# One change to a causal attention and int8 FFN layer on eight cores: how the last chunk of queries is cut, and what stands in its tail

## The reference, cut to what matters

```python
# x: (16, 2048, 1024) float32, 16 heads of 64
Q, K, V = heads(x @ WQ.T), heads(x @ WK.T), heads(x @ WV.T)
attn = softmax(where(causal, Q @ K.T / 8, -1e9)) @ V
x = layernorm(x + merge(attn) @ WO.T)            # eps 1e-5, over 1024
n = x * rsqrt(mean(x * x) + 1e-6)
q = clip(round(n * 127 / absmax(n)), -128, 127) * absmax(n) / 127   # per row
y = layernorm(x + (q @ (w_int8 * weight_scale).T + bias))
```

## Time and profile before

| | us |
|---|---|
| median of 3 runs (lowest, highest) | 1003.89 (1002.97, 1004.13) |
| the profiled execution's own time | 1004.11 |
| its span, slowest core (core 2) | 1002.6 |
| the other cores' spans | 994.9 to 1001.9 |

### The profile page before, as it was taken

How to read it: one execution, slowest core, us unless ns; L and a number is a source line. 1 busy time by engine, 2 the same in 40 slices (tenths; PEclk the granted TensorE clock), 3 DMA queues, 4 the chain that set the end, 5 groups by cost and what they waited for, 6 DMA issues and landing times.

```text
span 1002.6 us, 22536 instructions; the slowest of 8 cores (994.9 to 1002.6 us)
## 1 busy us (share of the span) xinstructions
PE 907.1 (90%) x8267; PEld 409.9 (41%) x8416; DVE 519.0 (52%) x1263; ACT 687.2 (69%) x713; POOL 227.4 (23%) x290
## 2 busy tenths in 40 slices
PE   3894999999999989999999999999799999999863
PEld 1342444444444433434444444444344444444421
DVE  0110147744786327653127747762477523776675
ACT  0133666776877789999744566777577779999931
POOL 5021322231122121221223232232122211222101
PEclk9997999999999999999999999999899999999897
DMA  9999333250223141221154251144413210114212
GB/s 117 146 178 182 65 45 42 64 147 13 28 64 101 54 53 28 79 44 62 37 66 66 64 148 23 33 107 94 49 33 102 74 44 10 25 26 146 62 56 63
DMA packets 99289, 71.18 MB, mean 71 GB/s; under 512 B 70384, under 2 KB 88816, under 8 KB 99184
## 3 DMA queue, kind: packets, MB, share of 16 engines
q1 hardware_dynamic: 78368, 50.87, 20.5%
q0 software_dynamic: 20816, 18.88, 14.8%
HBM read 55.05 MB, written 16.78 MB: 72 GB/s over the span
## 4 chain that ended last, share of the span: by engine, by line
PE 77%; DMA 8%; ACT 6%; issue 3%; DVE 3%; POOL 1%; DVEq 0%; POOLq 0%; ACTq 0%; SPq 0%
PE ps L324 47%; PE ps L640 16%; PE ps L531 14%; ACT PT L559 5%; DMA WV<-wvt 4%; DMA QO<-OS 2%; DMA XT<-xt 1%; DVE OS L682 1%; DMA QT<-QB 1%; POOL PT L574 1%; ACT Q L844 1%; POOL WK L148 0%; POOL WQ L148 0%; DVE SM L678 0%; DVE Z L749 0%
## 5 line engine op out<-in xcount | busy, mean ns | idle before, releaser
L559 ACT ACTIVATE PT<-ps,SM 128x1024 bf16<-128x1024 f32 (+2 forms) x576 | 586.2, 1066 | 151.8 <-PE ps L531 149.8
L574 POOL TENSOR_TENSOR PT<-PT,MASK 128x256 bf16<-128x256 bf16 (+1 forms) x184 | 158.2, 867 | 506.0 <-ACT PT L559 505.8
L640 PE MATMUL ps<-VX,PT 128*128 128x65 bf16 x4352 | 235.1, 195 | 25.4 <-DVE OS L682 22.6
L640 PEld LDWEIGHTS ps<-VX,PT 128*128 128x128 bf16 x4352 | 179.2, 98 | 177.0 <-issue 141.9
L531 PE MATMUL ps<-QO,KT 64*128 64x512 bf16 (+1 forms) x1504 | 193.3, 325 | 10.9 <-ACT PT L559 10.2
L324 PE MATMUL ps<-XT,WK 128*128 128x512 bf16 x486 | 126.0, 386 | 23.8 <-DMA XT<-xt 22.4
L324 PE MATMUL ps<-W,QT 128*128 128x512 bf16 x477 | 128.6, 385 | 17.5 <-DMA QT<-QB 13.8
L324 PE MATMUL ps<-WO,QO 128*128 128x512 bf16 x474 | 127.0, 378 | 4.2 <-issue 1.7
L324 PE MATMUL ps<-XT,WQ 128*128 128x512 bf16 x485 | 124.6, 380 | 2.5 <-DMA WQ<-wqt 1.1
L324 PE MATMUL ps<-WV,XT 128*128 128x512 bf16 x489 | 124.1, 383 | 2.7 <-DMA WV<-wvt 1.4
L531 PEld LDWEIGHTS ps<-QO,KT 64*128 64x128 bf16 x1504 | 51.7, 94 | 182.2 <-issue 177.3
(11 more groups left out here) (50 smaller groups left out, 546.5 us busy)
## 6 DMA issues: line engine op xcount, KB each, us to landing
Z<-x SPq DMA_DIRECT2D x32, 512.0 KB, 4.4
y<-Z SPq DMA_DIRECT2D x32, 512.0 KB, 2.8
XT<-xt POOLq DMA_DIRECT2D x7, 1024.0 KB, 12.5
WK<-wkt POOLq DMA_DIRECT2D x4, 512.0 KB, 21.4
WQ<-wqt POOLq DMA_DIRECT2D x4, 512.0 KB, 24.6
WV<-wvt POOLq DMA_DIRECT2D x2, 1024.0 KB, 42.2
WO<-wot POOLq DMA_DIRECT2D x1, 2048.0 KB, 70.6
W<-w8t POOLq DMA_DIRECT2D x1, 2048.0 KB, 87.1
```

What stands on the lines that cost most here:

```text
L559: emit("s", lambda eng: eng.activation(dst, src, AF.Exp, bias=EB, scale=0.125).then_inc(sem["s"], 1))
L574: emit("g", lambda eng: eng.tensor_tensor(blk, blk, msk, ALU.mult).then_inc(sem["m"], 1))
L640: last = eng.matmul(ps[:, o_at + s_ * o_head + q * 65: o_at + s_ * o_head + q * 65 + 65], PT[:, pt0 + s_ * 512 + c0: pt0 + s_ * 512 + c0 + ...
```

## The change

1. **Last chunk.** Chunk 7 becomes three stretches: 256, 128 and 128 queries. In a stretch of 128, a unit has four keys' blocks against 128 queries: S is 8 matmuls of 128 columns instead of 4 of 256. Such a stretch has 4 units for each pair of heads, 32 in all, so the chunk keeps 56 + 64 units. Its diagonal unit is the new kind `f`. The `ffn` and `wo` of tile 30 now also stand in the list of chunk 7, behind those of 28 and 29; only tile 31 is left for the tail.
2. **Fillers.** The list of chunk 7 is in another order, and its work is divided over 16 gaps fewer.
3. **Half-tile statistics, in all chunks.** BN_STATS, maximum and minimum of a half are put into `bg` as soon as that half of `wo` is done (`z_half`), and likewise BN_STATS of a half of `ffn` (`y_half`). Some of the planner's costs change (750 to 690, 1400 to 1200, 1100 to 350 + 160 nq).
4. **Last tile.** Its last scaling is done in two halves, one on ACT and one on DVE, with a store for each.
5. **Unread matmuls.** In the tail, PE gets 12 matmuls of 128x512 before tile 31's `wo` and 45 before its `ffn`; they write the score buffer and nobody reads them.

```diff
-        subs += [(NCH - 1, 0, 2), (NCH - 1, 2, 2)]
+        subs += [(NCH - 1, 0, 2), (NCH - 1, 2, 1), (NCH - 1, 3, 1)]
...
+                    kinds = ["f"] + list(range(first_k % 4, first_k, 4))
...
+            if nq == 1:
+                keys = ([k0] + list(range(k0 % 4)) if kd == "f"
+                        else list(range(kd, kd + 4)))
+                return [(k, j * 128, q0 * 128, 128)
+                        for j, k in enumerate(keys)]
...
-            dve_load(1100.0)
+            dve_load(350.0 + 160.0 * nq)
...
+        def z_half(n, j):
+            z = zt(n, j * 512, j * 512 + 512)
...
+            for f in (stats, high, low):
+                bg.append((690.0, lambda f=f: emit("v", f)))
...
-            part(0)
-            part(1)
...
-            if on_act:
+            if n == 4 * NCH - 1:
+                wait("s", tok_sm2[n])
+                emit("s", lambda eng: eng.activation(
+                    zt(n, 0, 512), zt(n, 0, 512), AF.Identity,
+                    bias=sm(n, 32, 33), scale=sm(n, 31, 32)).then_inc(
+                        sem["s"], 1))
+                t0 = bump("s")
+                wait("v", tok_sm2[n])
+                emit("v", lambda eng: eng.tensor_scalar(
+                    zt(n, 512, 1024), zt(n, 512, 1024), sm(n, 28, 29),
+                    sm(n, 31, 32), ALU.subtract, ALU.mult).then_inc(
+                        sem["v"], 1))
+                store(n, bump("v"), 512, 1024)
+                store(n, t0, 0, 512)
+            elif on_act:
...
+                if g == NCH - 1:
+                    order = [wo[0], wo[1], ff[0], wo[2], ff[1], wo[3],
+                             ff[2], ff[3]]
...
-                mine += behind([4 * g, 4 * g + 1])
+                mine = (mine[:4] + carry[:2] + mine[4:6] + carry[2:]
+                        + mine[6:])
+                carry = []
+                mine += behind([4 * g, 4 * g + 1]) + behind([4 * g + 2])
...
-            gaps = [todo]
+            gaps = [2 * len(pairs[g]) - (16 if g == NCH - 1 else 0)]
...
-        main.extend(behind([4 * NCH - 2, 4 * NCH - 1]))
+        main.extend(behind([4 * NCH - 1]))
+        def warm():
+            if idle[0] == 0:
+                wait("t", tok_exp[len(units) - 1], tok_exp[len(units) - 2])
+            idle[0] += 1
+            emit("t", lambda eng: eng.matmul(
+                ps[:, 0:512], WO[:, 0:128], WO[:, 0:512], start=True,
+                stop=True, skip_group_check=True))
         while main or st["open"] or timed or bg:
             if step() == 0.0:
-                spend(100.0)
+                if main and idle[0] < (12 if len(main) > 2 else 57):
+                    warm()
+                    spend(216.0)
+                else:
+                    spend(100.0)
```

More of the change, by code:

```diff
@@ L483, in build_nc @@
                     kinds = ["d0", "d1", "d2"] + list(range(first_k))
+                elif nq == 2:
+                    kinds = ["e"] + list(range(0, first_k, 2))
                 else:
-                    kinds = ["e"] + list(range(0, first_k, 2))
+                    kinds = ["f"] + list(range(first_k % 4, first_k, 4))
                 for kd in kinds:
@@ L551, in emit_s @@
             s0 = (u % 2) * 1024
-            if kd in ("d2", "e"):
-                c0, nc_ = (256, 256) if kd == "d2" else (0, 384)
+            if kd in ("d2", "e", "f"):
+                c0, nc_ = {"d2": (256, 256), "e": (0, 384),
+                           "f": (0, 128 * len(mm))}[kd]
                 dst = ap(PT, pt0 + c0, (4096, 128), (512, 2), (1, nc_))
@@ L586, in pv_lists @@
                 return [(k0, 1, 128)], [(k0, 0, 0), (k0 + 1, 1, 256)]
+            if nq == 1:
+                if kd == "f":
+                    return ([(k, 0, 128 + k * 128) for k in range(k0 % 4)],
+                            [(k0, 0, 0)])
+                return [(kd + j, 0, j * 128) for j in range(4)], []
             if nq == 2:
@@ L698, in o_out @@
             if hp == 7:
-                later(5500.0, lambda: state["ot_all"].add(su))
+                later(5500.0 if su < len(subs) - 1 else 3800.0, lambda: state["ot_all"].add(su))
         tok_x, tok_store, tok_sm, tok_q16, tok_qt8 = {}, {}, {}, {}, {}
@@ L713, in sm, with rows @@
             return SM[:, s0 + c0:s0 + c1]
-        def rows(t_h, n):
+        def rows(t_h, n, c0=0, c1=D):
             g, r = n // 4, n % 4
-            return ap(t_h, (g // 4) * S * D + ((g % 4) * 512 + r * 128) * D,
-                      (D, 128), (1, D))
+            return ap(t_h, (g // 4) * S * D + ((g % 4) * 512 + r * 128) * D
+                      + c0, (D, 128), (1, c1 - c0))
         def x_load(n):
@@ L752, in done @@
                 tok = bump("v")
+                z_half(n, dc)
                 if dc == 1:
@@ L758, in wo_filler, with stats, high, low @@
                           pieces, done)
+        def z_half(n, j):
+            z = zt(n, j * 512, j * 512 + 512)
+            def stats(eng):
+                eng.drain()
+                eng.bn_stats(sm(n, 16 + 6 * j, 22 + 6 * j), z)
+            def high(eng):
+                eng.tensor_reduce(sm(n, 2 + j, 3 + j), z, AX.X, ALU.max)
+            def low(eng):
+                eng.tensor_reduce(sm(n, 4 + j, 5 + j), z, AX.X, ALU.min)
+            for f in (stats, high, low):
+                bg.append((690.0, lambda f=f: emit("v", f)))
         def z_stats(n):
@@ L767, in col @@
                 return sm(n, j, j + 1)
-            def part(j):
-                z = zt(n, j * 512, j * 512 + 512)
-                def stats(eng):
-                    if j == 0:
-                        eng.drain()
-                    eng.bn_stats(sm(n, 16 + 6 * j, 22 + 6 * j), z)
-                def high(eng):
-                    eng.tensor_reduce(col(2 + j), z, AX.X, ALU.max)
-                def low(eng):
-                    eng.tensor_reduce(col(4 + j), z, AX.X, ALU.min)
-                for f in (stats, high, low):
-                    bg.append((750.0, lambda f=f: emit("v", f)))
-            part(0)
-            part(1)
             def f(eng):
@@ L912, in done @@
                 tok = bump("v")
+                y_half(n, dc)
                 if dc == 1:
@@ L918, in ffn_filler, with y_half, f @@
                           pieces, done)
-        def y_stats(n):
-            def part(j):
-                def f(eng):
-                    if j == 0:
-                        eng.drain()
-                    eng.bn_stats(sm(n, 16 + 6 * j, 22 + 6 * j),
-                                 zt(n, j * 512, j * 512 + 512))
-                bg.append((750.0, lambda: emit("v", f)))
-            part(0)
-            part(1)
+        def y_half(n, j):
+            def f(eng):
+                eng.drain()
+                eng.bn_stats(sm(n, 16 + 6 * j, 22 + 6 * j),
+                             zt(n, j * 512, j * 512 + 512))
+            bg.append((690.0, lambda: emit("v", f)))
+        def y_stats(n):
             def f(eng):
@@ L976, in store @@
             emit("y", lambda eng: eng.dma_start(
-                rows(y_h, n), zt(n)).then_inc(sem[key], 16))
+                rows(y_h, n, c0, c1), zt(n, c0, c1)).then_inc(sem[key], 16))
             tok_store[n] = bump(key, 16)
@@ L1095, in build_nc @@
             carry = late
-            todo = 2 * len(pairs[g])
-            gaps = [todo]
+            gaps = [2 * len(pairs[g]) - (16 if g == NCH - 1 else 0)]
             def gap():
@@ L1115, in build_nc @@
         pv_pair(npair - 1, gap)
-        main.extend(behind([4 * NCH - 2, 4 * NCH - 1]))
+        main.extend(behind([4 * NCH - 1]))
+        idle = [0]
+        def warm():
[5 more added lines that the diff above has]
+                stop=True, skip_group_check=True))
         while main or st["open"] or timed or bg:
             if step() == 0.0:
-                spend(100.0)
+                if main and idle[0] < (12 if len(main) > 2 else 57):
[3 more added lines that the diff above has]
+                    spend(100.0)
         for n in range(4 * NCH - NZ, 4 * NCH):
```

11 lines of the change are left out of this document (6 added, 5 removed).

## The result

The changed kernel is slower. Its median is 1010.7 us (5 runs), against 1003.66 us for five runs of the kernel before on the same chip. The ratio of the two is 1.0071, with a 95% interval of 1.0056 to 1.0085. The forecast was 1001.3 with a range of 996.5 to 1006.5: the sign and the range are both wrong. An interval stands in brackets. One of the five executions took 1101.72 us, with the cores of one die at a lower clock; such executions occur with and without the change, and they are counted in the medians here and in no ratio.

A forecast was written before the change was run, and what follows sets the result against it. PE and ACT nearly full in the last chunk, then a chain of dependent steps in the tail. Span 1002.6 - 13.8 (tail) + 11.7 (chunk 7) - 0.5 (statistics) = 1000.0, as a median 1001.3 us, range 996.5 to 1006.5.

The forecast's parts named there:

- Tail: After the last PV matmul: tile 31 alone remains, so the tail takes 29.3 us instead of 43.1, a gain of 13.8.
- Unread matmuls: In the tail: they hold the clock before tile 31's `ffn`, which without them would pay 3.2 us.
- Chunk 7: Last chunk: 48 moved filler matmuls cost 10.4 us, units without filler +0.8, clock 0.5; chunk longer by 11.7.
- the step that made +0.8: Chunk 7: PE time lost in units without filler, rising from 23 to 30, goes from 4.3 to 5.1 us.
- The 0.5 for the clock: Chunk 7: 0.5 us added for low clock around the longest row without filler, bounds 0 and 5.6.
- Narrow S, masks, head pairs at 0: Chunk 7: S in 128-column matmuls and eight more head pairs with masks and divisions add nothing.
- narrow S is bound by its instructions: Rival, chunk 7: S pays per instruction, +0.43 us on 38 units, 16 us; 1017 us, chance 0.02.
- the chunk swallows all of it: Rival, chunk 7: PE bound and narrow S dearer than wide; at 0.2 us per S 1008.9 us, chance 0.11.
- Half-tile statistics at -0.5, bounds -2 and +2: All chunks: DVE executes the same instructions, divisions stand less long behind statistics; -0.5 us in 72 head pairs.
- Cold tail: Rival, tail: unread matmuls come at half clock, 19 us, past the 11.8 when `ffn` is ready; +7, 1008 us, chance 0.05.
- No change: Rival, chunk 7: excess of 1 to 3 us from low clock or `ffn` queued before its transpose; 1003.5 us, chance 0.18.
- the chunk hides the work: Rival, chunk 7: the new order fills idle time counted as lost, chunk grows by 8; 997.5 us, chance 0.16.

The follow-up runs named there:

- e8: The changed kernel without the 57 unread matmuls in the tail; ratio 1.0110 to the kernel before, tail 34.0 us.
- e3: The changed kernel with half-tile statistics undone (both halves after the second `wo` half) and the old planner costs; ratio 1.0011 to the kernel before.
- e14: The changed kernel with half-tile statistics and changed planner costs only from chunk 7 on; ratio 1.0036 to the kernel before.
- e4: The kernel before with only chunk 7 cut into 256, 128 and 128 queries, last transpose estimate 3800 instead of 5500; ratio 1.0061, chunk 7 136.4 us.
- e11: The kernel before with all changed planner costs, and a tile ready for its `ffn` 6500 instead of 4000 after its transpose's issue; ratio 0.9990.

## Why the prediction was wrong

By its own steps, in their order:

- **Tail: right.** -13.8 forecast, -12.7 and -12.0 measured. Tile 31's statistics end 3.7 us behind its `wo` (3.0 forecast), the old 8.9 is gone. The chain on core 0 took 25.0 us from there to the end, 22.3 forecast. Of these 2.7, 1.7 are the last `ffn` at 5.30 instead of 3.61 and 0.7 the statistics.
- **Unread matmuls: nearly right in size, by luck.** 2.3 to 2.9 us (e8), 3.2 forecast, all of it for `ffn` at full clock. On most cores `ffn` lost the clock all the same, and 2.1 of the gain came at `wo`, for which I had counted nothing.
- **Chunk 7: the term was too small.** +11.7 forecast, +15.4 and +15.2 measured. The 10.4 for 48 matmuls at full speed is in it. What failed is the step that made +0.8 of 23 and 30 units without filler: "the first three of a row run ahead at 0.68 on the two buffers, which frees about 0.9 for each row of them". Only the first unit of a row ran ahead (in one of the five rows the third as well); 24 of 30 waited, 9.0 us, where the step left 5.1 (30 x 0.32 without its credit is 9.6). Before, 4.3 was nearly right (4.6) by luck, since the last four units of the long row came at low clock and did not wait. As a mean of eight cores the waits for the exponential rose by 3.1 and 3.3 us. The quantisations in the rows are a part of it that I had priced nowhere: waits above 0.6 us sum to 2.7 us instead of 2.1. The 0.5 for the clock is not borne out as a rise, by the mean clocks above. Some 1 to 2 us of PE's busy time beyond the 10.4 I can't place. Per moved matmul the chunk paid 15.4 / 48 = 0.32 us, and 0.27 in e3. At 0.32 the swap is 15.4 against 12.7: a loss of 2.7, and e14 measures one (1.0036).
- **Narrow S, masks, head pairs at 0: right** (pitch of 0.68, e4). The rivals "narrow S is bound by its instructions" and, in its mechanism, "the chunk swallows all of it" fall, though the second forecast the right sign and nearly the time (1008.9). That was luck: chunk growth passed its point of 14.3 by waits for ACT and not by the price of S, and the swap alone makes 1.0036 (e14), where this rival's time is 1.005. The 0.65 for a narrow S, which I had worked out from the Trainium skill ("TensorE: Matmul & The Clock Gate", Back-to-back issue gap), doesn't fit either: in the rows at 971.51 eight of them and eight PV matmuls with their loads take 0.68 together.
- **Half-tile statistics at -0.5, bounds -2 and +2: wrong, the larger miss.** +3.3 and +5.3 measured. The step that failed is "DVE is 52% busy and executes the same instructions". It treated the three costs as if they belonged to the statistics. They decide the order on all engines for 750 us. I had looked for the effect in the divisions, and PE's waits for them hardly moved (9.3 us and 9.7). What counted was PE, busy for 98.99 of 101.00 us in chunk 1 and bound to its order: its waits for `QT` are new (2.4 us, mean of eight), and e3 and e14, with part 3 left out of the body, have the body of before (750.4 and 750.0). The prediction argued from the order of chunk 7 and the tail, and from none of the body.
- **"Cold tail", "no change", "the chunk hides the work": wrong.** "No change" named the lump of 16 behind a long row, which is there, and `ffn` standing in PE's queue before its transpose has landed. That is there too, but it costs most in the body.

As I read it, both failed terms have one root: where PE is nearly full, its time depends on where each filler stands, and I priced fillers by their number.

What stays open: half of what the new costs do to the body (chunk 1 in e11), 1 to 2 us of chunk 7, and why five cores of eight get a low clock for the last `ffn` and three don't, after the same 45 matmuls and the same idle time. The three (3, 4 and 6) are also the only ones whose lump of 16 in chunk 7 ran at full clock.
